# The shared expert moves beside the choice of experts, and each expert's tile is scaled and added to the result's rows by an indirect transfer

## Chip, cores and metric

The kernel runs on one core of one Trainium2 chip. The metric is the device time of one execution in microseconds.

## The reference

A block of a transformer on 4 x 512 tokens of 512 values, all in float32. With `x` the tokens after a gated attention, which this change does not touch, the second half is a mixture of experts:

```
xn = layernorm(x)                                  # 2048 tokens x 512
scores = softmax(xn @ Wg.T)                        # 16 experts
keep the 2 best of 4 groups of experts, then the 4 best experts of those (weights = their scores)
y = sum over the 4 chosen experts of weight * (silu(xn @ W1.T) * (xn @ W3.T)) @ W2.T   # inner width 352
z = (silu(xn @ Ws1.T) * (xn @ Ws3.T)) @ Ws2.T      # shared expert, every token, inner width 704
out = x + tanh(g_ffn) * (y + z)
```

## The kernel before, in words

The stages follow each other, each in a block of its own that all engines leave before the next begins: projections and attention (0 to 596 us of the profile), then four that matter here.

`stage_close` (to 739 us) works in four batches of 512 tokens. SyncE loads the attention's output and its denominators (`c_den`), VectorE normalises, TensorE projects (L689), VectorE makes `x1` (L658) and the layer norm's `x2` (L673), TensorE transposes `x2` (L697) and makes the 16 logits per token. GpSimd's queue stores `x1` (L603), `x2` (L606) and, once both have landed, the transposed tokens `xT` (L610) to DRAM.

`stage_route` (739 to 809) is one long chain on VectorE with a wait after each instruction: softmax, best groups, best experts (`MAX8` per 128 tokens), and a place for each chosen pair of token and expert. The pairs are sorted by expert, each expert is padded to tiles of 128 rows, 79 tiles in all. Two small matmuls count (L918, L919). 64 matmuls (L927) with 79 columns each write the table `token` (which token stands in which row of which tile), from masks that VectorE makes. `slot` and `weight` say for each token where its four results will stand, and their weights.

`stage_experts` (809 to 1415) loops over the 79 tiles of 128 rows. GpSimd gathers the rows of `x2` four tiles ahead by an indirect transfer (L1071, after a copy of the tile's indices, L1068). TensorE transposes them (L1172), ScalarE rounds them to float32r and copies them (L1108, L1109), GpSimd subtracts to get the low part (L1076). Every product is made in three passes, high x high, high x low and low x high: `gate` and `up` (L1181, twelve matmuls each), the transposition of `h` (L1188), `yps` (L1200, nine). GpSimd also multiplies silu(gate) by up (L1088) and makes the low part of `h` (L1080). ScalarE copies the tile (L1121) and stores it to DRAM as `dy` (L1125). The weights of an expert (1.97 MB) are loaded by SyncE into one of two buffers once the last tile of the expert before the last is done (L1015 to L1019), and VectorE splits them into a high and a low part in nine pieces (L1044 to L1052). In its last part the stage also loads and splits the shared expert's weights (L1058, L1060).

`stage_combine` (1415 to the end) computes the shared expert in four batches: twelve matmuls for `gate` and twelve for `up` for each of six chunks of the inner width (L1375), then for each of four tiles of 128 tokens eighteen matmuls into `yps` (L1384). ScalarE and VectorE make `h` (L1311, L1331 to L1335). GpSimd gathers the four expert results of each token by indirect transfers (L1294). VectorE sums them with their weights, scales by tanh(g_ffn), adds `x1` (L1346, L1349), and SyncE stores a batch.

## Time and profile before

| | |
|---|---|
| median of three runs | 1698.18 us (1687.57 to 1803.11) |
| the profiled execution | 1688.83 us, of which its span is 1686.8 us |
| mean granted clock of TensorE | 0.870 of full speed |
| TensorE busy | 1348.6 us (80%) |
| VectorE, ScalarE, GpSimd busy | 755.0, 533.9, 613.2 us |
| moved | 194.97 MB |

"Busy" is the time in which at least one instruction of the engine runs. A granted clock of 1.0 is 2.4 GHz and one of 0.5 is 1.2 GHz. A stretch's clock is a mean over time, so 0.76 is a mix of the two levels. All times of rows count from the span's start.

### The profile page before, as it was taken

The numbers are of one execution on the slowest core, as the hardware profiler recorded it, in microseconds if no ns is written. First come the engines' busy times: TensorE is split into PE (matmuls) and PEld (weight loads), VectorE is DVE, ScalarE is ACT, GpSimd is POOL, SyncE is SP. The second block draws the span as 40 slices with busy tenths as digits, with TensorE's granted clock in tenths as the row PEclk, the third lists the DMA queues.
The fourth block names the chain that finished last, engine by engine and source line by source line (L and its number), as shares of the span: only waits on it lengthen the run. The fifth ranks groups of instructions, "written<-read, shape, count | busy, mean of one in ns | idle before, by whom it ended". The sixth has DMA issues, their size and how long they took to land. (4 is left out here: it accounts for less than half of the span.)

```text
span 1686.8 us, 28607 instructions
## 1 busy us (share of the span) xinstructions
PE 1348.6 (80%) x8380; PEld 965.6 (57%) x8381; DVE 755.0 (45%) x1939; ACT 533.9 (32%) x951; POOL 613.2 (36%) x810
## 2 busy tenths in 40 slices
PE   6566089889989836735399999999989995999996
PEld 3233064333333313435399998988888884675673
DVE  2112047888787314458503533443353520344343
ACT  1101015555555500110155554544444442100100
POOL 4111002333332200000267776775666774042232
PEclk9877589999898767855699999998999997998897
DMA  5434222333232154620344444443533533052342
GB/s 184 129 118 137 86 72 68 91 97 98 71 99 77 42 171 153 221 102 0 133 128 126 132 132 159 137 126 109 175 113 113 194 103 137 13 175 66 109 148 75
DMA packets 100017, 194.97 MB, mean 116 GB/s; under 512 B 27044, under 2 KB 28580, under 8 KB 98952
## 3 DMA queue, kind: packets, MB, share of 16 engines
q1 hardware_dynamic: 71400, 118.35, 21.9%
q0 software_dynamic: 17200, 55.38, 11.2%
q10 hardware_dynamic: 11376, 20.71, 3.2%
q8 instruction: 23, 0.38, 0.1%
q14 instruction: 18, 0.15, 0.0%
HBM read 130.07 MB, written 64.03 MB: 115 GB/s over the span
## 5 line engine op out<-in xcount | busy, mean ns | idle before, releaser
L421 DVE CUSTOM_DVE_ANT_0 a_mb<-a_mb,late 128x384 f32<-128x384 f32 (+3 forms) x512 | 244.1, 513 | 109.6 <-PE a_mb L458 102.2
L1044 DVE CAST e_w<-e_w 128x480 fp32r<-128x480 f32 x144 | 99.2, 699 | 319.2 <-DMA e_w<-in_w2T 319.1
L400 ACT ACTIVATE a_at<-a_eb 128x1024 f32<-128x1024 f32 (+3 forms) x256 | 178.5, 705 | 179.1 <-PE a_eb L476 179.1
L344 POOL TENSOR_SCALAR_AFFINE_SELECT a_at<-a_at 128x256 f32<-128x256 f32 x256 | 104.5, 408 | 331.1 <-ACT a_at L400 331.1
L1181 PE MATMUL e_gate<-e_w,e_xT 128*128 x948 | 178.0, 339 | 39.0 <-DVE e_w L1052 34.6
L1181 PEld LDWEIGHTS e_gate<-e_w,e_xT 128*128 128x128 f32 x948 | 165.2, 200 | 50.6 <-issue 39.8
L1200 PE MATMUL e_yps<-e_w,e_hT 128*128 x711 | 185.5, 404 | 1.9 <-ACT e_hT L1113 1.4
L1181 PE MATMUL e_up<-e_w,e_xT 128*128 x948 | 174.7, 334 | 0.0
L1181 PEld LDWEIGHTS e_up<-e_w,e_xT 128*128 128x128 f32 x948 | 154.2, 193 | 0.0
L490 PE MATMUL a_pv<-a_at,a_v 128*32 128x256 f32 (+3 forms) x2048 | 133.1, 335 | 14.5 <-POOL a_at L344 8.6
L1200 PEld LDWEIGHTS e_yps<-e_w,e_hT 128*128 128x128 f32 x711 | 128.1, 189 | 27.3 <-issue 1.6
L458 PE MATMUL a_mb<-a_k,a_q 49*128 49x256 f32 (+2 forms) x512 | 114.0, 442 | 14.1 <-DVE a_mx L421 4.1
L1080 POOL TENSOR_TENSOR e_hT<-e_hc,e_hT 128x384 fp32r<-128x384 f32 x79 | 86.1, 1090 | 101.3 <-ACT e_hc L1114 101.0
L1071 POOL DMA_INDIRECT e_x<-dx,e_idx x79 | 94.6, 1197 | 62.5 <-POOL e_idx L1068 62.5
L1048 DVE TENSOR_TENSOR e_w<-e_w 128x480 fp32r<-128x480 f32 x128 | 116.7, 912 | 0.0
L1076 POOL TENSOR_TENSOR e_xT<-e_xc,e_xT 128x512 fp32r<-128x512 f32 x79 | 109.8, 1390 | 8.8 <-ACT e_xc L1109 2.4
L1384 PE MATMUL s_yps<-ws,s_h 128*128 128x512 f32 (+1 forms) x288 | 103.7, 497 | 10.9 <-DVE s_h L1335 8.3
L476 PE MATMUL a_eb<-a_q,a_k 50*128 50x512 f32 x512 | 112.1, 434 | 0.0
L458 PEld LDWEIGHTS a_mb<-a_k,a_q 49*128 49x128 f32 x512 | 49.6, 190 | 94.7 <-DVE a_mx L421 87.7
L689 PE MATMUL c_op<-c_wo,c_on 128*128 128x512 f32 x128 | 61.6, 643 | 50.6 <-DVE c_on L637 29.9
L490 PEld LDWEIGHTS a_pv<-a_at,a_v 128*32 128x32 f32 x2048 | 42.5, 112 | 100.7 <-POOL a_at L344 54.5
L1088 POOL TENSOR_TENSOR e_h<-e_act,e_upc 128x352 f32<-128x352 f32 x79 | 83.4, 1056 | 32.1 <-ACT e_upc L1138 29.8
(194 smaller groups left out, 1785.7 us busy)
## 6 DMA issues: line engine op xcount, KB each, us to landing
e_w<-in_w13T SPq DMA_DIRECT2D x16, 1408.0 KB
dy<-e_y ACTq DMA_DIRECT2D x79, 256.0 KB
dq<-p_parts SPq DMA_DIRECT2D x48, 256.0 KB
a_q<-dq SPq DMA_DIRECT2D x64, 192.0 KB
do<-a_o SPq DMA_DIRECT2D x32, 256.0 KB, 3.5
dx<-c_x POOLq DMA_DIRECT2D x8, 1024.0 KB, 8.2
e_w<-in_w2T SPq DMA_DIRECT2D x16, 512.0 KB
a_k<-dk SPq DMA_DIRECT2D x64, 98.0 KB
```

The source lines that it names most:

```text
L344: eng.affine_select(out=square, in_=square, compare_op=ALU.is_ge, fill=0.0, base=0, pattern=[[0, 2], [1, P]], channel_multiplier=-1).then_ ...
L400: eng.activation(at[r % 2][:, ch, 2 * hp:2 * hp + 2, ch * P:SEQ], eb[hp][:, :, ch * P:SEQ], ACT.Exp, scale=0.25).then_inc(s_exp, 1)
L421: eng.tensor_tensor_reduce(out=b[:, 0:w], in0=b[:, 0:w], in1=io["late"][:, SEQ - w:SEQ], scale=1.0, scalar=3 * NEG, op0=ALU.add, op1=ALU.m ...
L458: eng.matmul(bank(place(turn, j, t))[:, 0:w], q[r][rows, j, ch * P:(ch + 1) * P], k[r][rows, 0:w], start=True, stop=True).then_inc(s_smax, 1)
L476: mm = eng.matmul(eb[j][:, t], k[r][rows, ch * P:(ch + 1) * P], q[r][rows, j, :], start=True, stop=True)
L490: mm = eng.matmul(pv[32 * h:32 * h + 32, cols], v[r][:, ch, :], at[r % 2][:, ch, 2 * j + t, cols], start=ch == 0 and part == 0, stop=ch == ...
L1044: eng.tensor_copy(w[rows, r, 0, cols], w[rows, r, 1, cols].bitcast(F32)).then_inc(s_high, 1)
L1048: eng.tensor_tensor(w[rows, r, 1, cols], w[rows, r, 1, cols].bitcast(F32), w[rows, r, 0, cols].bitcast(F32), ALU.subtract).then_inc(s_low, 1)
L1076: eng.tensor_tensor(xT[r][:, 1], xc[:], xT[r][:, 0].bitcast(F32), ALU.subtract).then_inc(s_xlow, 1)
L1181: mm = eng.matmul(out[r][:], xT[r][:, mine, k, :], w[:, bass.ds(buf, 1), its, at:at + INTER].rearrange("p b n -> p (b n)"), start=not (min ...
L1200: mm = eng.matmul(yps[:], hT[r][0:size, mine, n, :], w[0:size, bass.ds(buf, 1), its, at:at + D].rearrange("p b n -> p (b n)"), start=not ( ...
L1384: mm = eng.matmul(yps[j % 2][:], h[0:size, mine, n, j * P:(j + 1) * P], w2[0:size, its, n, :], start=not (mine or its or n), stop=mine == ...
```

## The change

- In `stage_close` ScalarE's queue loads the shared expert's three weight matrices, one after each of the first batches; ScalarE rounds each (`high_weights`), and GpSimd subtracts to get the low part (`low_weights`), behind the batch's stores.
- `stage_route` and `stage_combine` become one, `stage_shared`. VectorE runs the routing chain. TensorE computes the shared expert, with the two counting matmuls after the sixth chunk and the matmuls of the table two groups at a time after chunks 7 to 14. These now carry 158 columns, since the table holds the token and the scaled weight. In the down product the first five chunks of two result tiles come before the sixth. What VectorE did for the shared expert is done by ScalarE (`upc`, `h` high) and GpSimd (product, low parts, sum with `x1`). `x1 + tanh(g) * z` is stored to `out` in tiles of 256 KB. SyncE loads the first expert's weights at the stage's start, and the second's after all of these stores have landed. VectorE splits the first expert's weights at its chain's end.
- In `stage_experts` ScalarE scales each tile by its rows' weights as it copies it (`io["scale"]`), and GpSimd adds it to the rows of `out` with an indirect transfer that adds at its destination (`scatter`). That of tile g waits until that of g-1 has landed. Rows of padding go to 128 rows behind the result. GpSimd's loop is written out for all 79 tiles, without the copies of indices. The store of `dy`, the four gathers per token and the sums over four experts are gone. `y` has four buffers instead of two.

The core of the diff:

```diff
+def load_expert(eng, io, e, buf):
+
+    raw = io["w"][:, buf, SIDE:].bitcast(F32)
+    eng.dma_start(raw[:, 0:W13].rearrange("p (c n) -> p c n", c=KD),
+                  io["w13T"][bass.ds(e, 1)].rearrange("e (c p) n -> p (e c) n", p=P)).then_inc(io["s_w"], 16)
+    eng.dma_start(raw[:, W13:FULL].rearrange("p (c n) -> p c n", c=NI - 1),
+                  io["w2T"][bass.ds(e, 1), 0:(NI - 1) * P].rearrange("e (c p) n -> p (e c) n", p=P)).then_inc(io["s_w"], 16)
+    eng.dma_start(raw[0:REST, FULL:], io["w2T"][bass.ds(e, 1), (NI - 1) * P:INTER].rearrange("e p n -> (e p) n")).then_inc(io["s_w"], 16)
+
...
+            def high_weights(n):
+                high, _, raw = weights[n]
+                eng.wait_ge(s_ws, 16 * WS[n])
+                if n < 2:
+                    eng.activation(high, raw.bitcast(F32), ACT.Copy).then_inc(s_whigh, 1)
+                else:
...
+            eng.wait_ge(s_eps, 2)
+            for b in range(BATCH):
+                eng.wait_ge(s_mv, (b + 1) * CH + 1)
+                eng.activation(root[:], mv[:, :, 1], ACT.Sqrt, bias=eps[:]).then_inc(s_root, 1)
+                eng.wait_ge(s_keptT, b + 1)
+                for j in range(CH):
+                    eng.wait_ge(s_tr, b * CH + j + 2)
+                    eng.activation(x2T[:, :, j * P:(j + 1) * P], tp[j % 2][:], ACT.Copy).then_inc(s_xT, 1)
+                eng.wait_ge(s_lg, b + 2)
+                eng.activation(io["logits"][:, bass.ts(b, CH), :], lp[:], ACT.Copy).then_inc(s_lc, 1)
+                if b < 3:
+                    high_weights(b)
+                if b < 2:
+                    load_weights(b + 1)
...
+            def low_weights(n):
+                eng.wait_ge(s_whigh, n + 2)
+                high, low, raw = weights[n]
+                for rows, cols in ([(slice(0, P), slice(k * SHARED, (k + 1) * SHARED)) for k in range(KD)] if n < 2 else
+                                   [(slice(0, P), slice(k * D, (k + 1) * D)) for k in range(NS - 1)]):
+                    eng.tensor_tensor(low[rows, cols], raw[rows, cols].bitcast(F32), high[rows, cols].bitcast(F32), ALU.subtract).then_inc(s_wlow, 1)
...
+            for b in range(BATCH):
                 eng.wait_ge(s_x1, (b + 1) * CH + 1)
...
+                if b < 3:
+                    low_weights(b)
...
+            eng.tensor_scalar(indexf[:], tokps[:, 0:TILES], pad[:, 0:1], None, ALU.add).then_inc(s_v, 1)
...
+            eng.tensor_copy(io["scale"], tokps[:, TILES:]).then_inc(s_v, 1)
...
+            eng.wait_ge(io["s_w"], LOAD)
+            w = io["w"]
+            for n in range(CUTS + 1):
+                p, cols = cut(n)
+                eng.tensor_copy(w[p, 0, cols], w[p, 0, SIDE + cols.start:SIDE + cols.stop].bitcast(F32)).then_inc(s_high, 1)
+                eng.wait_ge(s_high, n + 2)
+                eng.tensor_tensor(w[p, 0, SIDE + cols.start:SIDE + cols.stop], w[p, 0, SIDE + cols.start:SIDE + cols.stop].bitcast(F32),
+                                  w[p, 0, cols].bitcast(F32), ALU.subtract).then_inc(s_low, 1)
 
...
+            def result(b, j):
+                i = b * CH + j
+                eng.wait_ge(s_down, i + 2)
+                if i >= 2:
+                    eng.wait_ge(s_sum, i)
+                eng.activation(part[i % 2][:], yps[i % 2][:], ACT.Copy, scale=tg[:, 0:1]).then_inc(s_part, 1)
...
+            for i, (b, n) in enumerate(units):
+                size = SCH[n][1]
+                eng.wait_ge(s_gate, i + 2)
+                eng.activation(act[i % 2][0:size], gate[i % 2][0:size], ACT.Silu).then_inc(s_act, 1)
+                eng.wait_ge(s_up, i + 2)
+                eng.activation(upc[i % 2][0:size], up[i % 2][0:size], ACT.Copy).then_inc(s_upc, 1)
+                eng.wait_ge(s_raw, i + 2)
+                if n == 0 and b:
+                    eng.wait_ge(s_down, b * CH + 1)
+                eng.activation(h[0:size, 0, n, :], raw[i % 2][0:size], ACT.Copy).then_inc(s_hhigh, 1)
+                if n == NS - 1:
+                    for j in range(CH):
+                        result(b, j)
+                        if j == 0 and b + 1 < BATCH:
+                            high_x(b + 1)
 
...
+            def add(b, j):
+                i = b * CH + j
+                eng.wait_ge(s_part, i + 2)
+                if j == 0:
+                    eng.wait_ge(s_x1, 16 * (b + 1))
+                eng.tensor_tensor(x1[:, j, :], part[i % 2][:], x1[:, j, :], ALU.add).then_inc(s_sum, 1)
+
+            low_x(0)
+            for i, (b, n) in enumerate(units):
+                size = SCH[n][1]
+                eng.wait_ge(s_act, i + 2)
+                eng.wait_ge(s_upc, i + 2)
+                eng.tensor_tensor(raw[i % 2][0:size], act[i % 2][0:size], upc[i % 2][0:size], ALU.mult).then_inc(s_raw, 1)
+                eng.wait_ge(s_hhigh, i + 2)
+                eng.tensor_tensor(h[0:size, 1, n, :], raw[i % 2][0:size], h[0:size, 0, n, :].bitcast(F32), ALU.subtract).then_inc(s_hlow, 1)
+                if n == NS - 1:
+                    for j in range(CH):
+                        add(b, j)
+                        if j == 0 and b + 1 < BATCH:
...
+            def multiply(i, n, m, out, done):
+                at, size = SCH[n]
+                for mine, its in PASSES:
+                    if mine and n == 0 and m == 0:
+                        eng.wait_ge(s_xlow, i // NS + 2)
+                    for k in range(KD):
+                        mm = eng.matmul(out[i % 2][0:size], weights[m][its][:, k * SHARED + at:k * SHARED + at + size],
+                                        xT[:, bass.ds(side[mine], 1), k, :].rearrange("p b n -> p (b n)"),
+                                        start=not (mine or its or k), stop=mine == 1 and k == KD - 1)
+                mm.then_inc(done, 1)
+
+            def down(b, j, chunks):
+                i = b * CH + j
+                for mine, its in PASSES:
+                    for n in chunks:
+                        size = SCH[n][1]
+                        first = its * DOWN + n * D
+                        mm = eng.matmul(yps[i % 2][:], h[0:size, mine, n, j * P:(j + 1) * P],
+                                        io["w"][0:size, bass.ds(side[1], 1), first:first + D].rearrange("p b n -> p (b n)"),
+                                        start=not (mine or its or n), stop=mine == 1 and n == NS - 1, skip_group_check=True)
...
+            def table(t):
+                r = t % 2
+                eng.wait_ge(s_row, 3 * t + 4)
+                for k in range(NK):
+                    mm = eng.matmul(tokps[:], at_row[r][:, k, :], at_col[r][:, k].rearrange("p n g -> p (n g)"), start=t == 0 and k == 0,
+                                    stop=t == NT - 1 and k == NK - 1, skip_group_check=True)
+                mm.then_inc(s_tok, 1)
+
+            for i, (b, n) in enumerate(units):
+                if n == 0:
+                    eng.wait_ge(s_xhigh, b + 2)
+                if i >= 2:
+                    eng.wait_ge(s_act, i)
+                multiply(i, n, 0, gate, s_gate)
+                if i >= 2:
+                    eng.wait_ge(s_upc, i)
+                multiply(i, n, 1, up, s_up)
+                if i == NS - 1:
+                    eng.wait_ge(s_ch, 2)
+                    eng.matmul(flat(within), io["before"], flat(chosen[:]), start=True, stop=True).then_inc(s_mm, 1)
+                    eng.matmul(flat(totals), io["onesb"], flat(chosen[:]), start=True, stop=True).then_inc(s_mm, 1)
+                if NS <= i < NS + NT // 2:
+                    for t in range(2 * (i - NS), 2 * (i - NS) + 2):
+                        table(t)
+                if n == NS - 1:
+                    early, late = tuple(range(NS - 1)), (NS - 1,)
+                    eng.wait_ge(s_hlow, i + 1)
+                    for j in range(2):
+                        if b or j >= 2:
+                            eng.wait_ge(s_part, b * CH + j)
+                        down(b, j, early)
+                    eng.wait_ge(s_hlow, i + 2)
+                    for j in range(2):
+                        down(b, j, late)
+                    for j in range(2, CH):
+                        eng.wait_ge(s_part, b * CH + j)
+                        down(b, j, early + late)
+
+        @block.sync
+        def _(eng):
+            def load_xT(b):
...
+            load_xT(0)
+            eng.dma_start(gf[:], io["gf"].broadcast_to([P, 1])).then_inc(s_g, 16)
+            load_expert(eng, io, 0, 0)
+            for b in range(BATCH):
+                if b:
+                    eng.wait_ge(io["s_base"], 16 * CH * b)
+                eng.dma_start(x1, dram["x1"][bass.ts(b, SEQ), :].rearrange("(j p) d -> p j d", p=P)).then_inc(s_x1, 16)
+                eng.wait_ge(s_up, (b + 1) * NS + 1)
+                if b + 1 < BATCH:
+                    load_xT(b + 1)
+                for j in range(CH):
+                    eng.wait_ge(s_sum, b * CH + j + 2)
+                    eng.dma_start(out[bass.ts(b * CH + j, P), :], x1[:, j, :]).then_inc(io["s_base"], 16)
+            eng.wait_ge(s_down, NT + 1)
+            eng.wait_ge(io["s_base"], 16 * NT)
+            load_expert(eng, io, 1, 1)
...
+            def gather(g):
+                n = g % XB
+                eng.indirect_dma_start(out=x[n][:], out_offset=None, in_=dram["x2"],
+                                       in_offset=bass.IndirectOffsetOnAxis(ap=io["gather"][:, g:g + 1], axis=0)).then_inc(s_x[n], 16)
+
+            def scatter(g):
+                n, last = g % XB, (g - 1) % XB
+                eng.wait_ge(s_y, g + 2)
+                if g:
+                    eng.wait_ge(s_out[last], 16 * ((g - 1) // XB + 1))
+                else:
+                    eng.wait_ge(io["s_base"], 16 * NT)
+                eng.indirect_dma_start(out=out, out_offset=bass.IndirectOffsetOnAxis(ap=io["scatter"][:, g:g + 1], axis=0),
+                                       in_=y[n][:], in_offset=None, compute_op=ALU.add).then_inc(s_out[n], 16)
 
...
+            for g in range(TILES):
+                r = g % 2
+                if g:
                     low_h(g - 1, 1 - r)
                 eng.wait_ge(s_upc, g + 2)
                 eng.wait_ge(s_act, g + 2)
                 eng.tensor_tensor(h[r][:, 0:INTER], act[r][:], upc[:], ALU.mult).then_inc(s_h, 1)
-                if exists(g + 1):
+                if g < LAST:
                     low_x(g + 1, 1 - r)
-                if exists(g + XB):
+                if g >= 2:
+                    scatter(g - 2)
+                if g + XB < TILES:
                     eng.wait_ge(s_xt, g + 2)
-                    gather(g + XB, n)
-
-            for g in range(XB):
-                gather(g, g)
-            for r in range(2):
-                eng.memset(h[r][:, INTER:], 0.0).then_inc(s_pad, 1)
...
+                eng.activation(y[n][:], yps[:], ACT.Copy, scale=io["scale"][:, bass.ds(g, 1)]).then_inc(s_y, 1)
```

## Rows read from the trace of the kernel before

The times in a timeline are start and duration in us; in brackets stands how long the engine sat idle before, and what ended it. In the table by stage the columns are the window, its length, each engine's busy us (instructions), the granted clock, the DMA engines' share and GB/s.

**Rows 1.** Table by stage: close, route, experts, combine.

```profile
607.00:739.00 132.00, 90.20 (x320) 53.05 (x320) 52.37 (x116) 16.33 (x29) 8.31 (x12) 0.77 0.51 185
739.00:809.00 70.00, 28.55 (x132) 28.06 (x132) 56.71 (x224) 1.70 (x2) 0.67 (x5) 0.50 0.00 0
829.00:1415.00 586.00, 550.02 (x3156) 509.58 (x3156) 216.94 (x279) 272.06 (x551) 388.43 (x386) 0.97 0.39 128
1427.00:1687.00 260.00, 237.20 (x864) 163.62 (x864) 112.65 (x156) 19.83 (x28) 64.72 (x73) 0.89 0.32 105
```

**Rows 2.** Timeline, end of the routing stage.

```profile
807.81 0.24 DVE L906 CAST token<-r_tokps 128x79 int32<-128x79 f32 x1
```

**Rows 3.** Timeline, start of the experts' stage.

```profile
811.67 1.06 POOL L1071 DMA_INDIRECT e_x<-dx,e_idx  x1 [0.94 <-POOL e_idx L1068]
...
818.91 1.11 PE L1172 MATMUL e_xps<-ident,e_x 128*128 128x128 f32 x4 [13.84 <-DMA e_x<-dx,e_idx]
...
829.50 0.95 PE L1181 MATMUL e_gate<-e_w,e_xT 128*128 x2 [9.47 <-DVE e_w L1052]
```

**Rows 4.** Table of waits, closing stage: total us, times, longest.

```profile
DVE c_on L637 <- DMA c_den<-dinv: 54.9, 3, 19.1
```

**Rows 5.** Timeline of GpSimd around one tile of the experts.

```profile
1007.79 1.01 POOL L1071 DMA_INDIRECT e_x<-dx,e_idx  x1 [0.79 <-POOL e_idx L1068]
1009.93 1.01 POOL L1080 TENSOR_TENSOR e_hT<-e_hc,e_hT 128x384 fp32r<-128x384 f32 x1 [1.12 <-ACT e_hc L1114]
...
1012.30 1.29 POOL L1076 TENSOR_TENSOR e_xT<-e_xc,e_xT 128x512 fp32r<-128x512 f32 x1
...
1014.51 1.01 POOL L1071 DMA_INDIRECT e_x<-dx,e_idx  x1 [0.79 <-POOL e_idx L1068]
```

**Rows 6.** Timeline, one load and split of an expert's weights.

```profile
1013.43 0.38 SPq L1015 DMA_DIRECT2D e_w<-in_w13T  x1
...
1023.82 1.14 DVE L1044 CAST e_w<-e_w 128x480 fp32r<-128x480 f32 x2 [20.14 <-DMA e_w<-in_w2T]
...
1026.20 1.50 DVE L1044 CAST e_w<-e_w 128x480 fp32r<-128x480 f32 x1
...
1028.19 0.40 DVE L1044 CAST e_w<-e_w 128x480 fp32r<-128x480 f32 x1
...
1037.21 1.08 PE L1181 MATMUL e_gate<-e_w,e_xT 128*128 x5 [3.88 <-DVE e_w L1052]
```

**Rows 7.** Table of waits, experts' stage.

```profile
PE e_gate L1181 <- DVE e_w L1052: 34.6, 8, 9.5
```

**Rows 8.** Timeline of GpSimd, end of the closing stage.

```profile
724.70 0.75 POOL L603 DMA_DIRECT2D dx<-c_x  x1 [4.66 <-issue]
...
735.20 0.55 POOL L610 DMA_DIRECT2D dxT<-c_x2T  x1 [4.65 <-DMA dx<-c_x]
```

**Rows 9.** Chain that ended last, order of time, last stage: start, us, what.

```profile
1418.73 6.35 DMA s_gf<-in_gf
...
1427.15 4.67 PE s_gate L1375 x12
...
1434.54 2.72 PE s_gate L1375 x12
...
1523.34 27.29 PE s_yps L1384 x72
...
1674.46 3.68 DMA s_got<-dy,s_idx
```

**Rows 10.** Table by windows, one down phase of the shared expert.

```profile
1523.00:1551.00 28.00, 27.66 (x74) 16.07 (x75) 13.65 (x17) 0.01 (x1) 8.74 (x10) 0.76 0.24 65
```

**Rows 11.** Groups of instructions, last stage, TensorE.

```profile
L1384 PE MATMUL s_yps<-ws,s_h 128*128 128x512 f32 (+1 forms) x288 | 103.7, 497 | 10.9 <-DVE s_h L1335 8.3 <-DVE s_h L1333 2.6
```

**Rows 12.** DMA issues: median us to landing last.

```profile
do<-a_o SPq DMA_DIRECT2D x32, 256.0 KB, 3.5
```

**Rows 13.** Timeline of ScalarE, end of the experts' stage.

```profile
1411.02 0.60 ACT L1121 ACTIVATE e_y<-e_yps 128x512 f32<-128x512 f32 x1 [2.15 <-PE e_yps L1200]
```

500 lines of the change are left out of this document (189 added, 311 removed).

## The prediction

> **What bounds the kernel now.** I read the stretches by stage first, then the waits inside each, then a few timelines. In the table by stage [rows 1] the reader is to see that TensorE is nearly always busy in the experts' stage (550 of 586 us) and in the last stage, which holds the shared expert and the combination (237 of 260 us), and nearly idle in the routing stage (28.6 of 70 us, at half the clock). So the time of the two big stages is the time of their matmuls, and the 70 us of routing are a chain of small VectorE instructions that hides nothing. Its last instruction, the copy of the table of tokens, comes at 807.81, 69 us into the stage [rows 2]. Behind it the first gather needs from 811.67 to 818.91 to land, and the first expert's gate waits until 829.50 for split weights [rows 3]. The stage before routing waits for transfers [rows 4].
>
> In the experts' stage the rhythm is that of one tile: two gathers start 6.72 us apart [rows 5]. Seven times, besides the start, an expert's weights come late: loading starts at 1013.43, has landed at 1023.82, and the gate that uses it starts at 1037.21 after 3.88 us of idleness [rows 6]; with the start it is 34.6 us in 8 waits [rows 7].
>
> **The change, part by part.** The sum is made against the profiled span, 1686.8 us.
>
> *Closing stage: +14.* The shared weights are now loaded (4.1 MB), rounded by ScalarE and split by GpSimd in this stage. The loads compete with the reads for which VectorE already waits 54.9 us in three batches [rows 4]. At the 185 GB/s of this stretch [rows 1] 4.1 MB are 22 us if all of it lay on the path; nothing if it fits between. I take 4. The third split stands on GpSimd ahead of the last batch's two stores. It is five pieces of 128x512 and one smaller, at 1.29 us each [rows 5] 7.7 us, behind ScalarE's rounding, some 2 us more. The store that went out at 724.70 [rows 8] goes out at about 734.5, and the last one of the stage, at 735.20, depends on it. That is +10; zero would need another cover, and I see none, since GpSimd was already the last to issue. Bounds for the part: 0 to +25.
>
> *Routing and start of the experts: −90.5.* From 739 to 829.5 nothing of the old order is left on TensorE's path. VectorE's chain runs beside the shared expert. It needs its 70 us, some 15 us more for the waits for TensorE (the counting matmul now stands behind the sixth chunk), and a split of 9 us, and has 250. The longest cover in this change is that one; if it failed, the tables would come late and TensorE would stand.
>
> *The shared expert in its new place: +250.6.* Stage start 3 us, then 10 us until transposed tokens are loaded and rounded: in the old stage the first loads were under way at 1418.73 and the gate starts at 1427.15 [rows 9]. 48 groups of twelve matmuls at 2.72 us [rows 9] are 130.6, plus 2 for the first at the low clock (4.67 instead of 2.72). The down phase took 27.3 us for 72 matmuls [rows 9], at a mean granted clock of 0.76 [rows 10]: half of it at 1.2 GHz, and each of the four begins after 2.7 us of idleness, 10.9 in all [rows 11]. The new order puts the first five chunks of two result tiles in front, so that this idleness goes; at the full clock the phase is 27.3 x 0.76 = 20.7 us, four are 83. If the clock stays as it was, they are 109. The table matmuls move in here: 128 instructions took about 28 us at half the clock [rows 1]. They now carry 158 columns instead of 79. Between 14 (twice the clock) and 28 I take 20, with 2 for small waits. Sum: 13 + 130.6 + 2 + 83 + 20 + 2.
>
> GpSimd now does the shared expert's product and its low part, 2 x 1.29 us in each 5.44 us of a chunk, and ScalarE three passes; both are hidden. Rows show that VectorE and GpSimd slow each other: the same cast takes 1.50 us at 1026.20 and 0.40 at 1028.19 [rows 6]. The Trainium skill, "SBUF — State Buffer", section "Who interferes with whom", says that a VectorE instruction with two SBUF inputs contends with GpSimd's reads, and this change puts routing beside GpSimd's work on purpose. By that rule doubled GpSimd times would be 5.2 of 5.44 us in a chunk, still covered, and the first split of the tokens would come about 5 us later: the sum would be 5 us higher. I leave it out, since the row behind it is of another mix.
>
> *Handing over to the experts: +18.7.* After TensorE's last matmul come scaling (0.6, as the copy in [rows 13]), the addition (1.3 [rows 5]), a store of 256 KB, which in this profile lands after 3.5 us [rows 12], its issue and those of the second expert's load (1.7), because SyncE waits for all stores before it issues that, and the next stage's start (2.6). Then the gather's 7.2 us [rows 3] and 1.8 to a rounded tile. The first expert's weights are split by then, which is why the 10 us between 818.91 and 829.50 go.
>
> *The experts' loop: 581.5 becomes 606.5.* On ScalarE the issue of the store disappears. On GpSimd the copy of an index and the 0.79 us for which the gather waits for it [rows 5] disappear, and one indirect transfer of 1.01 us comes. Issue alone is about even. New is the wait in front of it: the scatter of tile g−2 waits until that of g−3 has landed. Behind it on GpSimd stand the gather four tiles ahead and the low part of h, for which TensorE's down product waits. GpSimd waits 1.12 us for ScalarE there today [rows 5], so with the slack behind it a scatter may take some 8 us from its issue once, but in the long run no more than the 6.72 of a tile. No row shows an adding transfer. The nearest are an indirect read of the same size, landed 3.68 us after its issue at the end [rows 9], and 7.2 us beside a weight load [rows 3]. With reading and writing of its destination I put it at 5 to 5.5 alone and 9 to 10 beside a load. Alone it is hidden; beside each of 14 loads one or two lie over the limit, about 1 us each time after the slack: 15. The destination is read too, so the load itself lasts longer, about 1.4 us, and seven experts already wait for theirs: 10. Bounds: 0 (both hidden) to several hundred (the rival below).
>
> The Trainium skill, "DMA: Bandwidth & Descriptors", section "Anatomy of one DMA", fits a GpSimd transfer as 2.0 us plus bytes over 436e3, which is 2.6 us for 256 KB; it has no figure for an adding one. With that the 15 us would vanish and the sum be 15 lower; the trace's 3.68 is already longer.
>
> *The end: 275.8 removed, 9 added.* From TensorE's last expert matmul, for which ScalarE waits until 1411.02 [rows 13], to the end stood the whole last stage. Now: the last tile is scaled (0.6), the scatter before it must have landed, then its own issue and landing, 1 + 5.5, and the stage's close.
>
> Sum: 739 + 14 + 250.6 + 18.7 + 606.5 + 9 = 1637.8. Outside the span the profiled run had 2.0 us, so 1640. The profiled run (1688.8) is near the lowest of the three shown and 0.6% below their median, 1698.2; a median of the new kernel may lie as much above its own profile. Halfway between, I say 1645. A measurement of this kernel can tell about 2% from no change.
>
> **The rivals.**
> *The chain of scatters sets the pace (slower).* Each scatter waits for the one before, so if one takes L us from issue to landing and L is over 6.72, the tile takes L. At 8.7 us, 79 tiles cost 158 us, of which 25 are counted: 1640 + 133 = 1773. For it: the transfers must read, add and write 2 KB rows, and beside loads even a plain gather took 7.2. Against it: 3.68 us alone, and a plain 256 KB store 3.5. It decides exactly at 6.72 us. 0.16.
>
> *The weights come too late everywhere (no change).* If the adding transfers lengthen every load by 5 us, seven short experts wait 5 more, and the seven of five tiles or more, which have about 3.5 us to spare (four tiles at 6.72, less 10.4 of loading and 13 of splitting), wait 1.5 and run 1.6 at the low clock: some 57, of which 10 are counted: 1687. For it: 10.4 of the about 27 us between loading and use go to the load already. 0.15.
>
> *The overlap is worse than it looks (no change).* The down phase stays at 0.76 (+26) and the tables at 28 (+8): 1674. Against it: the idleness in front of the phase, after which the clock was low, is filled. 0.04.
>
> *Everything hidden (faster still).* No cost in the closing stage and none in the loop: 1640 − 14 − 25 = 1601. 0.20.
>
> **How the numbers follow.** The forecast, 1625 to 1665, gets 0.45. A tenth of it lies within 2%. Faster by over 2%: 0.40 + 0.20 = 0.60. Within 2%: 0.05 + 0.15 + 0.04, about 0.23. Slower: 0.17, the chain. The range is 1595 to 1720; it leaves out the chain and a little of the edges.
>
> **What would show it.** Right: TensorE busy from about 765 to 1005 with the clock near full in the down phases, VectorE's tables done before 920, experts' gates from about 1025, GpSimd's waits for a scatter only beside loads. Wrong: a tile's rhythm above 6.8 us with GpSimd's scatter waiting for the transfer each time; more than 4 us of waiting at each new expert; a closing stage that ends after 765; waits of TensorE for the tables.

## The result, and the profile after

The new kernel took **1645.14 us** (median of 4, 1636.26 to 1649.12), the kernel before 1694.57 (median of 4) on the same chip: ratio **0.9714**, 95% interval 0.965 to 0.9779. The ratio is of the fast executions alone; one of the kernel before, 1803.11 us, was slow. The profiled execution took 1647.19 us with a span of 1645.3. A second series on another chip gave 1649.14, ratio 0.9796 (0.9725 to 0.9867): faster too, but by an amount that its interval puts between 1.3 and 2.8%.

The profile was read like that of before: stages, then what ends the waits in each. Table by stage, new kernel: close, shared expert beside the choice, experts (columns as in [rows 1]).

```profile
600.00:753.00 153.00, 92.13 (x320) 53.84 (x320) 62.61 (x116) 19.98 (x30) 30.80 (x26) 0.72 0.53 187
763.00:1004.00 241.00, 233.42 (x994) 174.01 (x994) 104.53 (x224) 63.37 (x95) 102.13 (x68) 0.97 0.16 56
1017.00:1632.00 615.00, 564.41 (x3156) 513.49 (x3156) 210.49 (x265) 272.79 (x553) 476.19 (x390) 0.95 0.50 115
```

The two stretches that [rows 1] shows as routing (70 us, TensorE 28.6 busy) and last stage (260) are one of 241 us in which TensorE is busy for 233. In the experts' stage, against [rows 1], GpSimd's busy time has gone from 388 to 476 us of some 600 and TensorE's clock from 0.97 to 0.95, and the stage has grown by 30 us: that is the row to explain.

GpSimd at the end of the closing stage, timeline; it answers to [rows 8].

```profile
734.94 6.14 POOL L677 TENSOR_TENSOR e_w<-e_w 128x512 fp32r<-128x512 f32 x5 [6.20 <-ACT e_w L649]
741.05 1.44 POOL L681 TENSOR_TENSOR e_w<-e_w 64x512 fp32r<-64x512 f32 x1
742.44 0.79 POOL L686 DMA_DIRECT2D dx<-c_x  x1
...
750.11 0.55 POOL L692 DMA_DIRECT2D dxT<-c_x2T  x1 [5.15 <-DMA dx<-c_x]
```

The third split stands for 7.6 us ahead of the store, which is issued 17.7 us later than in [rows 8], the last one 14.9 later. But the two profiles don't start the stage at the same time. Its first load, kernel before and new kernel, timeline:

```profile
593.76 0.34 SPq L579 DMA_DIRECT2D c_sums<-do  x1
587.10 0.34 SPq L613 DMA_DIRECT2D c_sums<-do  x1
```

The work ahead of the stage, which the change does not touch, was 6.7 us shorter in the new kernel's profile. From this load to the last store it is 141.4 us before and 163.0 after: the closing stage has grown by 21.6 us, and 14.9 is what is left of it on the clock of the span. The wait of [rows 4], new kernel:

```profile
DVE c_on L706 <- DMA c_den<-dinv: 78.7, 4, 22.3
```

A down phase of the shared expert, new kernel, table by windows: clock 1.00, where [rows 10] had 0.76. TensorE's 72 matmuls take 19.5 us instead of 27.3.

```profile
929.00:949.50 20.50, 20.41 (x78) 13.55 (x77) 0.00 (x0) 5.54 (x7) 10.94 (x6) 1.00 0.25 90
```

From the shared expert to the first expert, timeline, new kernel; it answers to [rows 3].

```profile
1002.07 0.69 ACT L1035 ACTIVATE s_part<-s_yps,s_tg 128x512 f32<-128x512 f32 x1 [4.67 <-PE s_yps L1118]
...
1010.67 1.06 POOL L1270 DMA_INDIRECT e_x<-dx,gather  x1 [6.58 <-POOLq L75]
...
1015.78 1.12 PE L1375 MATMUL e_xps<-ident,e_x 128*128 128x128 f32 x4 [13.75 <-DMA e_x<-dx,gather]
...
1017.78 2.71 PE L1384 MATMUL e_gate<-e_w,e_xT 128*128 x8 [0.88 <-DVE e_w L1259]
...
1018.16 5.71 POOL L1285 TENSOR_TENSOR e_xT<-e_xc,e_xT 128x512 fp32r<-128x512 f32 x1 [2.44 <-ACT e_xc L1322]
...
1023.93 1.54 PE L1384 MATMUL e_gate<-e_w,e_xT 128*128 x4 [3.44 <-POOL e_xT L1285]
```

The gather ends a wait of 13.75 us, and then GpSimd's low part, 5.71 us instead of 1.3 while VectorE splits weights, holds the gate's last matmuls up for 3.44 us.

GpSimd around one tile of the experts, timeline, new kernel; it answers to [rows 5].

```profile
1206.62 1.02 POOL L1289 TENSOR_TENSOR e_hT<-e_hc,e_hT 128x384 fp32r<-128x384 f32 x1
1207.59 0.94 POOL L1303 TENSOR_TENSOR e_h<-e_act,e_upc 128x352 f32<-128x352 f32 x1
1208.49 1.27 POOL L1285 TENSOR_TENSOR e_xT<-e_xc,e_xT 128x512 fp32r<-128x512 f32 x1
1209.93 1.59 POOL L1280 DMA_INDIRECT out<-e_y,scatter  x1 [0.17 <-issue]
1211.83 1.00 POOL L1270 DMA_INDIRECT e_x<-dx,gather  x1 [0.30 <-issue]
...
1225.36 1.72 POOL L1280 DMA_INDIRECT out<-e_y,scatter  x1 [2.48 <-DMA out<-e_y,scatter]
```

In [rows 5] GpSimd waited 1.12 us for ScalarE and 0.79 for an index; over the stage it was 101.0 us in 69 tiles and 59.2 in 75. Here the five instructions follow each other with at most 0.3 us between them: this tile of 6.7 us is full. Over the whole loop GpSimd is busy for 78%, and it still waits 33.0 us for ScalarE ahead of the low part of h, in 17 tiles. The scatter's issue takes 1.59 us, and beside a load it waited 2.48 for the one before it.

The table of waits in the experts' stage (against [rows 7]):

```profile
POOL out L1280 <- DMA out<-e_y,scatter: 38.3, 14, 3.0
PE e_gate L1384 <- DVE e_w L1259: 19.9, 8, 4.5
PE e_yps L1403 <- POOL e_hT L1289: 17.3, 14, 1.4
```

TensorE waits less for weights (19.9 us; 34.6 before) and in exchange for the low part of h, which stands behind the scatter. The tiles that this touches are those beside a load. Taken between starts of GpSimd's product, half of all tiles are no longer than 6.72 us, in the kernel before (6.71) as in the new one; but 30 are over 7.2 us, where it was 10. A late split, timeline (against [rows 6]):

```profile
1228.11 4.29 DVE L1259 TENSOR_TENSOR e_w<-e_w 128x480 fp32r<-128x480 f32 x1
...
1234.99 3.81 DVE L1250 CAST e_w<-e_w 128x480 fp32r<-128x480 f32 x1
...
1242.41 3.88 PE L1384 MATMUL e_gate<-e_w,e_xT 128*128 x12 [4.49 <-DVE e_w L1259]
```

Two of VectorE's instructions take some 4 us instead of 0.40 and 0.65. Each covers one unbroken run of GpSimd's three arithmetic instructions (from 1228.77 to 1231.88, and from 1235.40 to 1238.52; such a run fills 1206.62 to 1209.76 above). The 14 whole splits of the loop take 14.6 us in the mean, where they took 13.5. The end, timeline, and the summary of all scatters:

```profile
1629.84 0.69 ACT L1334 ACTIVATE e_y<-e_yps,scale 128x512 f32<-128x512 f32 x1 [2.17 <-PE e_yps L1403]
1631.60 1.57 POOL L1280 DMA_INDIRECT out<-e_y,scatter  x1 [2.84 <-DMA out<-e_y,scatter]
1637.15 1.57 POOL L1280 DMA_INDIRECT out<-e_y,scatter  x1 [3.98 <-DMA out<-e_y,scatter]
```

```profile
L1280 POOL DMA_INDIRECT out<-e_y,scatter x79: 1568/1595/1861, 1044.9 to 1637.1; - x79
...
DMA to landing us min/median/max: 4.6/4.9/8.8
```

### The profile page after: what moved, and what is told of

It is laid out like the page before. It is cut to its first block and busy times, and to the rows that moved or that the text cites. A ratio compares the mean times of both kernels' runs of the same rounds, so it can differ in the third digit from the quotient of the medians.

```text
span 1645.3 us, 27429 instructions
## 1 busy us (share of the span) xinstructions
PE 1324.6 (81%) x8378; PEld 949.2 (58%) x8379; DVE 689.4 (42%) x1765; ACT 577.0 (35%) x1016; POOL 755.5 (46%) x812
## 5 line engine op out<-in xcount | busy, mean ns | idle before, releaser
L1250 DVE CAST e_w<-e_w 128x480 fp32r<-128x480 f32 x135 | 93.7, 703 | 421.4 <-DMA e_w<-in_w2T 421.4
L1384 PE MATMUL e_gate<-e_w,e_xT 128*128 x948 | 184.1, 346 | 30.2 <-DVE e_w L1259 19.9
L1403 PE MATMUL e_yps<-e_w,e_hT 128*128 x711 | 189.1, 407 | 18.3 <-POOL e_hT L1289 17.3
L1384 PEld LDWEIGHTS e_gate<-e_w,e_xT 128*128 128x128 f32 x948 | 167.5, 203 | 46.9 <-issue 37.4
L1280 POOL DMA_INDIRECT out<-e_y,scatter x79 | 130.7, 1654 | 56.1 <-DMA out<-e_y,scatter 42.3
L521 PE MATMUL a_pv<-a_at,a_v 128*32 128x256 f32 (+3 forms) x2048 | 129.6, 327 | 15.1 <-POOL a_at L375 8.6
L1259 DVE TENSOR_TENSOR e_w<-e_w 128x480 fp32r<-128x480 f32 x135 | 136.6, 1020 | 0.0
L1270 POOL DMA_INDIRECT e_x<-dx,gather x79 | 85.1, 1077 | 30.0 <-issue 22.1
L1289 POOL TENSOR_TENSOR e_hT<-e_hc,e_hT 128x384 fp32r<-128x384 f32 x79 | 81.5, 1031 | 34.3 <-ACT e_hc L1327 33.0
L1334 ACT ACTIVATE e_y<-e_yps,scale 128x512 f32<-128x512 f32 x79 | 54.4, 689 | 112.9 <-PE e_yps L1403 112.9
```

The lines of the kernel that those rows point to most:

```text
L521: mm = eng.matmul(pv[32 * h:32 * h + 32, cols], v[r][:, ch, :], at[r % 2][:, ch, 2 * j + t, cols], start=ch == 0 and part == 0, stop=ch == ...
L1250: eng.tensor_copy(w[rows, r, cols], w[rows, r, SIDE + cols.start:SIDE + cols.stop].bitcast(F32)).then_inc(s_high, 1)
L1259: eng.tensor_tensor(w[rows, r, rest], w[rows, r, rest].bitcast(F32), w[rows, r, cols].bitcast(F32), ALU.subtract).then_inc(s_low, 1)
L1280: eng.indirect_dma_start(out=out, out_offset=bass.IndirectOffsetOnAxis(ap=io["scatter"][:, g:g + 1], axis=0), in_=y[n][:], in_offset=None, ...
L1384: mm = eng.matmul(out[r][:], xT[r][:, mine, k, :], w[:, bass.ds(buf, 1), its * SIDE + at:its * SIDE + at + INTER].rearrange("p b n -> p (b ...
L1403: mm = eng.matmul(yps[:], hT[r][0:size, mine, n, :], w[0:size, bass.ds(buf, 1), its * SIDE + at:its * SIDE + at + D].rearrange("p b n -> p ...
```

## The experiments

Profiled executions differ by up to 28 us in when the closing stage starts, in work that no experiment touches. So stretches are compared: *shared* is from TensorE's first gate of the shared expert to its last down matmul, *loop* from the first expert's first gate to the last down matmul, *handover* between these, *tail* from the loop's end to the span's. Each is taken between starts of matmuls. Loops of kernels with the same loop came out between 604 and 614 us; less than 10 us there is no verdict. Most experiments ran once. Four of them (e2, e3, e4, e7) leave out, or do twice, a part of the result's sum, and e10 works with stale low parts: they measure and are no kernels to keep.

| run | shared | handover | loop | tail | time (runs) |
|---|---|---|---|---|---|
| the changed kernel | 234.1 | 16.3 | 611.6 | 15.9 | 1645.14 (4) |
| a0_new | 233.9 | 16.3 | 611.0 | 14.8 | 1649.14 (4) |
| e1_tables_first | 212.1 | 16.4 | 608.1 | 14.6 | 1690.23 (1) |
| e5_down_in_order | 271.3 | 16.4 | 604.1 | 14.5 | 1673.90 (1) |
| e6_split_last | 234.5 | 16.3 | 604.3 | 14.6 | 1643.51 (5) |
| e8_gather_early | 232.3 | 10.6 | 610.9 | 14.4 | 1655.07 (1) |
| e2_two_results | 234.5 | 17.0 | 594.1 | 9.4 | 1623.46 (1) |
| e3_plain_store | 234.0 | 16.4 | 588.4 | 6.1 | 1624.74 (1) |
| e4_twice | 232.2 | 16.4 | 894.5 | 30.5 | 1953.97 (1) |
| e7_no_add | 232.2 | 16.4 | 590.5 | 11.0 | 1638.97 (1) |
| e10_less_low | 232.3 | 16.3 | 580.4 | 14.8 | 1616.80 (1) |
| e11_scatter_earlier | 232.2 | 16.4 | 647.1 | 13.4 | 1692.64 (10) |
| e9_both | 232.3 | 10.6 | 614.3 | 14.6 | 1640.74 (6) |

The kernel before had a loop of 581.1.

**The changed kernel again** (a0_new), beside the first experiments.

> The new kernel again, on the chip of the next three. Both theories: within 0.5% of its first profile, a span of 1637 to 1653 us. The stretches to compare with: closing stage until its last store is issued at 750, shared expert's matmuls from 767 to 1002, the experts' from 1018 to 1630.

It agreed in every stretch, to 1.1 us.

**Is hiding the route the gain?** (e1_tables_first)

```
     for i in range(NS + NT // 2 ...):      # TensorE's units of the shared expert
-        if i == NS - 1: wait s_ch; matmul within, totals
-        if NS <= i ...: table(t)
+    # all of it ahead of the loop: wait s_ch; matmul within, totals; table(t) for t in range(NT)
```

> TensorE makes the counts and the whole table before the first chunk of the shared expert, so that the routing chain again stands in front of everything. Theory (the gain is mainly the chain of small VectorE instructions, now hidden): TensorE starts the shared expert 75 to 85 us later, saves the 19 us of table matmuls among the chunks, and the time rises by 55 to 65 us, to about 1705, nearly all of the way back to the kernel before. Rival (the gain comes from the gathers, sums and idle gaps of the old last stage, and the chain would cost little): under 20 us.

TensorE started the shared expert 66.5 us later than in a0_new (837.1 against 770.6), the shared stretch shrank by 21.8, and the first expert's gate came 44.8 us later. The rival, under 20, fell; the theory was some 10 too high. The overlap is worth about 45 us, as much as the whole gain of the change. Of the 21.8 us only some 17 are the tables' matmuls. The rest is the start of the shared expert: its first two groups of twelve take 6.69 and 3.95 us behind idleness in the changed kernel, and 3.06 and 2.96 here, behind the tables.

**Does the order of the down phase keep the clock?** (e5_down_in_order)

```
-  early, late = tuple(range(NS - 1)), (NS - 1,)
-  wait s_hlow i+1;  down(b, 0, early), down(b, 1, early);  wait s_hlow i+2;  late of 0, 1;  then 2, 3
+  wait s_hlow i+2;  down(b, j, tuple(range(NS))) for j in 0..3
```

> The down product of the shared expert takes its six chunks in order for each tile, with no early part in front of the wait for the last chunk. Theory: TensorE idles some 4 us before each of the four down phases (two passes on ScalarE and two on GpSimd), the granted clock of the phase falls to about 0.76 as in the kernel before, and each batch costs 4 + 6 us: +35 to +42 in all. Rival (the clock is not lost through that gap, the old phases were slow for another reason, as the sums on VectorE): only the gaps, +14 to +18, and a clock above 0.9 in the phases.

The shared stretch grew by 37.4 us, as the theory had it. Table by windows, the third down phase of this run with the wait ahead of it:

```profile
941.00:970.00 29.00, 24.93 (x75) 14.55 (x75) 0.00 (x0) 5.39 (x7) 10.89 (x6) 0.88 0.17 63
```

The third phase itself and the last one, timeline of this run:

```profile
945.17 24.48 PE L1118 MATMUL s_yps<-e_w,s_h 128*128 x72 [4.07 <-POOL s_h L1084]
1007.50 30.04 PE L1118 MATMUL s_yps<-e_w,s_h 128*128 x72 [4.07 <-POOL s_h L1084]
```

TensorE waited 14.1 us for the last chunk's h in four waits, and was busy 23 us longer over the whole stage (256.4 against 233.4) for the same matmuls at a lower clock. The four waits were 3.9, 2.0, 4.07 and 4.07 us, and the phases behind them took 23.0, 23.0, 24.5 and 30.0 us, at a mean granted clock of 0.93, 0.93, 0.86 and 0.67; in the changed kernel each takes 19.5 or 19.6. So a wait and its phase together cost 9 us in the mean, but from 5 to 15, and the 0.76 of the theory is not one value that every phase has.

**The split ahead of the stores** (e6_split_last)

```
     after batch b's stores of dx and dxT:
-    if b < 3: low_weights(b)
+    if b < 2: low_weights(b)
+    if b == 3: low_weights(2)       # behind the last store of dxT
```

> The split of the third shared matrix on GpSimd stands behind the last batch's stores in the closing stage, not in front of them. Theory (it is that split that makes the stage end some 9 us later): the last store of the stage goes out 8 us earlier and the whole gains 6 to 9 us, about 0.5%. Rival (the added weight loads and the slowed VectorE set the end of the stage): 0 to 2 us.

From the stage's first matmul to the last store of dxT it is 129.0 us instead of 133.8 in the changed kernel (127.9 in e9_both), but from there to the shared expert's gate 21.3 instead of 17.3 (20.7 in e9_both). Together it is 150.3 us, and 148.6 in e9_both, where the kernels whose closing stage is as in the changed one lie between 150.2 and 154.1: a gain of 3 us at most, and in e6 none that can be told. Timeline of this run, what stands there now:

```profile
768.02 0.55 POOL L692 DMA_DIRECT2D dxT<-c_x2T  x1 [4.38 <-DMA dx<-c_x]
768.59 6.14 POOL L677 TENSOR_TENSOR e_w<-e_w 128x512 fp32r<-128x512 f32 x5
774.69 1.25 POOL L681 TENSOR_TENSOR e_w<-e_w 64x512 fp32r<-64x512 f32 x1
779.81 0.34 SPq L1167 DMA_DIRECT2D s_xT<-dxT  x1
```

The next stage's first load goes out at 779.81, 11.8 us behind the last store instead of 8.1 in the changed kernel: the split is now the last work that the block of the closing stage has to wait for. In total 1643.51, ratio 0.9732 (0.9664 to 0.9799), not to be told from the changed kernel. The expected 6 to 9 was a miss.

**The gather in the handover** (e8_gather_early)

```
+  # stage_shared, GpSimd, behind the addition of the last batch's second tile:
+  wait s_low 2;  four gathers into io["ex"] (x laid over shared weights no longer used)
+  # VectorE: wait s_xlow 2 ahead of the second expert's split;  gathers leave the experts' stage
```

> The first four gathers are issued by GpSimd in the shared stage, behind its second last additions, into a part of the shared weights that is dead by then, and VectorE's split of the second expert waits until the first tile's low part is made. Theory (the handover of 16 us between the last down product and the first gate holds 5 us of gather latency and its queueing, and the first low part takes 5.7 instead of 1.3 us beside the split): the first gate starts 4 to 6 us earlier and the second pass does not wait 3.4 us, -7 to -10 us. Rival (the store and the load in front of the stage's end are the handover, the gather hides behind them): 0 to 3 us.

The handover is 5.7 us shorter, the 4 to 6 of the theory's first half; the wait on VectorE gave nothing more, since another of the first tiles' low parts came late instead (TensorE waited 4.2 us in all). The single time of 1655.07 says nothing of this: its closing stage started 16 us later than in the changed kernel.

**Who pays in the experts' loop: two destinations** (e2_two_results)

```
-  wait scatter(g - 1) landed;  out=out
+  wait scatter(g - 2) landed;  out=dram["out2"] if g % 2 else out     # base stored to both
```

> Scatters of odd tiles go to a second array of the result's shape, which is not added to the result; each scatter waits for the last but one and not for the one before. The base is stored to both. Theory (beside a weight load a scatter lands after 8.8 us, over the 6.7 of a tile, and GpSimd's wait for it delays the low part of h): the 17 us that TensorE waits for that low part vanish, and the loop shortens by 14 to 22 us, with the splits of weights unchanged. Rival (GpSimd is late by its work, 1.6 us for each scatter, and the wait only fills the gap): under 5 us.

Waits of TensorE, this kernel, loop:

```profile
PE e_gate L1386 <- DVE e_w L1260: 37.3, 10, 5.5
...
PE e_yps L1405 <- POOL e_hT L1291: 0.4, 1, 0.4
```

GpSimd's wait for a landing is gone and so is TensorE's for the low part of h (17.3 to 0.4); the loop is 17 us shorter, as the theory had it, and the rival fell. The scatter still takes 1.59 us to issue, and the splits are as long as before or longer (14.8 us). The tiles over 7.2 us go from 30 to 13. Weights come late more often (37.3 us against 19.9): part of what TensorE waits for the low part of h in the changed kernel comes back here as waiting for weights.

**No scatters** (e3_plain_store)

```
-  GpSimd: scatter(g - 2)
+  ScalarE: dma_start(dram["y"][tile g], y[n])          # as before
```

> No scatter: each scaled tile is stored in order to an array of its own from ScalarE's queue, as in the kernel before, and not added to the result. This measures all that the scatters cost in the loop. Theory (32 us longer than before, through waits of GpSimd and through VectorE's splits, which last 14.9 instead of 13.6 us beside a busier GpSimd): the experts' loop takes 580 to 585 us as before, splits 13.6, and 8 us more are saved at the end, -35 to -42 in all. Rival (the loop is longer for another reason, such as instructions written out 79 times or the first tiles): the loop stays above 600.

Loop −23 and tail −10, so −33 where −35 to −42 was expected; splits take 12.6 us. The other 7 us of the loop against the kernel before are not the scatter, and too few to be told from nothing. Beside e2 this says one thing more: without the wait for landings the loop is 594.1 us, and without the scatter altogether 588.4. The issue of 79 scatters, 1.60 us each, is worth 6 us of the loop at most, less than the 10 that can be told.

**Two scatters per tile** (e4_twice)

```
+  again(g - 3) behind low_h:  wait s_out 32*(..)+16;  the same adding transfer a second time
```

> Each tile is added twice, the second time by a scatter that waits for the first and for which the next tile's first one waits. It stands between the two products of GpSimd. Theory (the chain of scatters is hidden as long as it is shorter than a tile and sets the pace above that): a tile takes twice 4.9 us and a little, 9.8 to 10.5, the loop 775 to 830 us, +160 to +220. Rival (scatters overlap in part or only their issue counts): 1.6 us more a tile at most, +130 or less.

GpSimd in two tiles of this kernel, timeline:

```profile
1300.82 1.59 POOL L1280 DMA_INDIRECT out<-e_y,scatter  x1 [1.85 <-DMA out<-e_y,scatter]
...
1305.97 1.58 POOL L1286 DMA_INDIRECT out<-e_y,scatter  x1 [1.21 <-DMA out<-e_y,scatter]
...
1311.50 1.59 POOL L1280 DMA_INDIRECT out<-e_y,scatter  x1 [1.78 <-DMA out<-e_y,scatter]
```

These start 5.2 and 5.5 us behind the one before. In the loop all but one of the scatters waited for the landing of the one before; from start to start it is 5.4 us in the middle and 5.7 in the mean, and up to 11 beside loads. The tile takes 11.3 us in the mean, and the kernel 1954. Both theories were below that (the loop 283 us longer instead of 160 to 220). So a chain of scatters does set the pace once it is longer than a tile. With one scatter per tile of 6.7 us and a link of 5.4 to 5.7 the prediction's rival is about 1 us away. The second scatter also stands in the place that e11 below shows to be a bad one, so not all of the 283 us need be the chain's.

**What adding costs** (e7_no_add)

```
-  in_=y[n][:], in_offset=None, compute_op=ALU.add)
+  in_=y[n][:], in_offset=None)
```

> The same scatters in the same chain, which overwrite the rows and do not add. Theory (reading the destination is a small part of the 4.9 us, issue and landing the rest): landing 3.7 to 4.4 us alone and 7 to 8 beside a load, issue still 1.6; the loop 3 to 12 us shorter. Rival (the adding form is what makes both issue and landing slow): issue falls to the gather's 1.0 us, landing to 3.7, the loop gains 20 us or more.

Summary of this kernel's scatters:

```profile
L1280 POOL DMA_INDIRECT out<-e_y,scatter x79: 968/1029/1284, 1062.9 to 1629.4; - x79
...
DMA to landing us min/median/max: 2.7/2.8/7.2
```

The adding form costs 0.57 us more to issue and 2.1 more to land. The loop falls by 20.5 us, the rival's size; my theory that this part is small fell. It is no more than 4 us beyond e2, which kept the slow issue.

**Is it the landing, or is GpSimd full?** e3 and e7 shorten both the issue and the landing; e2 took away the wait alone. This one gives GpSimd time and leaves the scatters alone (e10_less_low).

```
   # low_x, from the third tile on
-  tensor_tensor(xT[r][:, 1], xc, xT[r][:, 0], subtract)
+  some = slice(0, 1);  tensor_tensor(xT[r][:, 1, some], xc[:, some], xT[r][:, 0, some], subtract)
```

> From the third tile on, GpSimd makes only a quarter of the tokens' low part (128x128 instead of 128x512; the rest stays what it was two tiles earlier); scatters, their waits and everything on the other engines stay. GpSimd gets back some 1.0 us of each 6.7 us tile. Theory (GpSimd has no slack: between 1199.2 and 1221.6 of the changed kernel its five instructions follow each other with waits of 0.3 us at most, so that the 1.60 us issue of a scatter, not only its landing, is what fills the engine, and what a landing takes is not won back): the loop falls from 611 to 592 to 600 us, TensorE's waits for the low part of h from 19 to under 8. Rival (only the landing beside a load counts, and VectorE's splits): the loop stays within 5 us of 611, with the same waits of GpSimd for the landing and TensorE's waits for the low part of h as before, 15 to 20.

Table of waits, this kernel, loop:

```profile
POOL e_hT L1290 <- ACT e_hc L1328: 54.3, 50, 4.5
POOL out L1280 <- DMA out<-e_y,scatter: 35.7, 13, 3.1
PE e_gate L1385 <- DVE e_w L1259: 24.1, 13, 3.0
...
PE e_yps L1404 <- POOL e_hT L1290: 4.3, 13, 0.6
```

The loop takes **580.4 us, that of the kernel before**, while GpSimd waits for landings as long as it did (35.7 us in 13 waits; 35.5 in 13 in the changed kernel's loop). What changed is that GpSimd waits for ScalarE again (54.3 us; 33.0 in the changed kernel, 101.0 before), so a late landing is won back before TensorE needs the low part of h. So a late landing alone costs nothing; it costs where GpSimd has no time to win it back. The theory had this, but not the size: the loop fell by 31 us and not by 11 to 19. The splits also went from 14.6 to 13.2 us, and the clock from 0.95 to 0.98. Half of the 31 us is TensorE's idleness (47.6 to 32.2 us), half its busy time (564.4 to 548.5): the granted clock is at its low level for 17 us of this loop, for 38 in the kernel before, and for 51 to 56 in the changed kernel, in e2, in e7 and in e3, which has no scatter at all. The run takes off arithmetic that the kernel before had too (0.8 us of GpSimd per tile, measured, not the 1.0 expected), so its 31 us are not the price of the scatter. How much of them is time won back and how much VectorE's shorter splits it doesn't separate.

**Where the scatter stands** (e11_scatter_earlier)

```
   for g: low_h(g - 1)
+         scatter(g - 2)
          product(g);  low_x(g + 1)
-         scatter(g - 2)
          gather(g + 4)
```

> Only the order on GpSimd changes: the scatter of tile g-2 stands behind the low part of h of tile g-1 and ahead of the product of tile g, instead of behind the low part of the next tokens. What then stands behind a late landing is the product, for which a transposition waits, and no longer the low part of h. Theory (the in-line position decides whom a late landing holds up): TensorE's waits for the low part of h fall from 19 to under 8, those for the product rise by less than that, and the loop is 3 to 10 us shorter than 611. Rival (GpSimd has no slack wherever the scatter stands, so that a wait of 2 to 3 us arrives at TensorE in any order): the waits only change their name, and the loop stays at 605 to 615, the time within 0.5% of the changed kernel's.

Both theories fell, though TensorE's waits for the low part of h are gone as the first had it: the loop is 36 us longer, and the kernel is back at the time of before (ratio 0.9985, 0.9944 to 1.0026). Its waits, and GpSimd in one tile:

```profile
POOL e_hT L1289 <- ACT e_hc L1327: 131.9, 79, 7.4
PE e_gate L1384 <- POOL e_xT L1285: 42.6, 63, 2.5
```

```profile
1215.21 1.48 POOL L1289 TENSOR_TENSOR e_hT<-e_hc,e_hT 128x384 fp32r<-128x384 f32 x1 [0.91 <-ACT e_hc L1327]
1216.85 1.59 POOL L1280 DMA_INDIRECT out<-e_y,scatter  x1 [0.16 <-issue]
1217.92 1.50 POOL L1305 TENSOR_TENSOR e_h<-e_act,e_upc 128x352 f32<-128x352 f32 x1
1218.83 1.82 POOL L1285 TENSOR_TENSOR e_xT<-e_xc,e_xT 128x512 fp32r<-128x512 f32 x1
```

GpSimd isn't even full here, it waits 0.9 us or more for ScalarE in every tile. By its waits, the scatter now stands inside a ring: low part of h, product, low part of the next tokens, then TensorE's gate, which waits for it in 63 of 79 tiles. In the changed kernel the scatter stands behind the low part of the tokens, where only the gather follows, which is four tiles early. The same instructions in another order on one engine cost 36 us of loop.

**The two mends together** (e9_both: e6 and e8)

> The late split in the closing stage and the early gathers together. Theory: the gains add up, -13 to -18 us, 0.8 to 1.1% faster than the new kernel. Rival: one of them hides the other or comes to nothing, under 0.5%.

1640.74 us, ratio 0.9745 (0.97 to 0.9791). The handover kept its 5.7 us and the closing stretch its 3, but the total can't be told from the changed kernel's, and the 13 to 18 us did not come.

## Why the prediction came out as it did

By its own terms, ends measured against the predicted ones (stage ends taken as the prediction took them, the closing stage 3.8 us behind its last store):

| term | predicted | measured |
|---|---|---|
| closing stage | +14 | +14.9 |
| shared expert in its new place | 250.6 | 248.2 |
| handover | 18.7 | 15.7 |
| experts' loop | 606.5 | 612.1 |
| end | 9 | 15.5 |
| span | 1637.8 | 1645.3 |

*Closing stage: right on the span's clock by luck.* Against its own start the stage has grown by 21.6 us, not 14.9, since the work ahead of it was 6.7 us shorter in this profile. The split ahead of the stores is 7.6 us, as worked out, but taking it away shortens the stretch up to the last store by only 5 to 6 us, and the next stage starts at most 3 us earlier (e6, e9). So most of the 21.6 is not the split: from the first matmul to the last store it was 116.6 us before, 133.8 in the changed kernel, and still 129.0 in e6. For the competition of the weight loads I took 4 us (of 0 to 22), and this is the term with the largest miss of this part. That it is the loads is read from VectorE's wait for `c_den`, 78.7 us for 54.9, since the weight loads are what is new on the queues beside it; no run took them away.

*Shared expert: right in sum and in mechanism, its parts less so.* Tables cost 18.5 us for 20. Down phases took 77.9 us for 83, at a clock of 1.00. The 48 groups of gate and up took 139 us for 132.6, because the first two ran at the low clock (6.69 and 3.95 us; 4.67 and 2.88 before). The 109 us for down phases that keep the old clock went by one phase; the four of the kernel before took 23.0, 27.3, 27.4 and 25.9 us, the 103.7 of [rows 11]. The mechanism, that the idleness ahead of the phase sets its clock, is shown by e5; that the route is hidden, by e1. The Trainium skill's rule on VectorE and GpSimd ("SBUF — State Buffer", section "Who interferes with whom"), which the prediction weighed and left out here, cost TensorE next to nothing in this stage: the gate waited 0.8 us for GpSimd's low part. The trace agrees with the rule itself, with VectorE as the one that waits. While GpSimd makes that low part (from 767.37, for 4.54 us), a small instruction of the routing chain takes 4.42 us, where one of the same form takes 0.21 at 774.3, and the chain has time for it. Timeline, new kernel:

```profile
767.56 4.42 DVE L883 TENSOR_TENSOR r_gtmp<-r_gm 128x48 f32<-128x48 f32 x1
```

*Handover: 3 us less.* From the gather's issue to the transposition it was 5.1 us, not the 7.2 of [rows 3]. That same rule does show right behind it, 5.71 us instead of 1.3 for the first low part, which my sum had nowhere; it lies in the loop, 3.4 us.

*The loop: the landings right, the loads wrong.* The sum had 25 us, 15 for landings and 10 for slower loads; the loop grew by 30.6. Landings of 4.9 us alone and 8.8 at most beside a load were as predicted (5 to 5.5, 9 to 10), and so was their path: TensorE's waits for the low part of h are 17.3 us for the 15 said, and e2, which takes the wait for landings away, shortens the loop by 17. The term that is wrong is the 10 for slower loads: loads are 0.6 us longer instead of 1.4, and TensorE waits 15 us less for weights, not 10 more. e2 shows why: once TensorE is not held up by the low part of h, its waits for weights rise from 19.9 to 37.3 us. In place of the 10 stand 7 to 13 us that are left without a wait (e2: 594.1, e3: 588.4, before: 581.1), of which the record doesn't show the cause.

"Issue alone is about even" was put too simply, though it is not what cost the time. An adding scatter takes 1.60 us to issue, not the 1.01 of a gather, and what it replaced was mostly idleness (59.2 us for indices; and the waits for ScalarE fell from 101.0 to 33.0). In tiles away from a load it is even: the middle tile is 6.72 us long, as before. But the idleness was the reserve that a late landing is won back from, and the "slack behind it" of the prediction was mostly gone. e10 gives some of it back, and the landings, as late as ever, cost TensorE 4.3 us instead of 17.3. So it takes both, a late landing and an engine without reserve. VectorE's splits, held by GpSimd's unbroken runs, take 14.6 us instead of 13.5; e2 is 17 us shorter with splits as long, so they are not the larger part. In all TensorE is 14 us longer busy (564 against 550, clock 0.95 for 0.97) and 16 longer idle.

*The end: 6.5 us more.* The prediction let the scatter before the last have landed for nothing. Two stand back to back, 5.55 us apart; from the last one's issue to the end it is 8.2.

*The number.* That 1645 was said and 1645.14 measured is luck to this precision. The forecast put 5 us for the median on top of its sum, where the measured median lies 2 us below its own profile; the shorter work ahead of the closing stage gave 6.7 us; and the parts above err in both directions. The parts from the closing stage on are 14 us over their sum.

*The rivals.* The chain did not decide, with 6.72 us against 5.4 to 5.7 for a link; e4 shows that it would have, and e11 that a place in the wrong ring costs 36 us without any longer transfer. "Weights too late everywhere" is excluded by the row of 19.9 us, "the overlap is worse than it looks" by the clock of 1.00 in the down phases, and "everything hidden" by the 21.6 us of the closing stage and the 30.6 of the loop.

What stays open: the 7 to 13 us by which the loops of e3 and e2 are longer than that of before, which is near what can be told; what the weight loads alone cost the closing stage; and whether a low part of x made elsewhere, all of it, would keep e10's gain, which wasn't tried.

## What to carry to other kernels

When an instruction is added to an engine that serves others, count its idleness per tile before and after and not only its busy share: what it waited for was the reserve that swallowed late transfers (e10). When two profiles are compared stage by stage, take each stage from its own start: here the work ahead of it differed by 6.7 us. Put an instruction that may wait behind the last one on its engine that anybody needs in this tile, and ahead of one that is early anyway. Idle stretches of a few microseconds ahead of a block of matmuls can cost more than their length, because the clock falls behind them: here waits of 2 to 4 us were followed by blocks that took 3.4 to 10.5 us longer (e5).

## What the runs showed of the hardware

- An indirect scatter of 128 rows of 2 KB that adds at its destination takes 1.60 us of GpSimd to issue and lands after 4.9 us (8.8 at most, beside a weight load); the same without adding takes 1.03 and 2.8 (7.2). Back to back, each waiting for the last, the adding ones start 5.4 us apart in the middle, 5.7 in the mean.
- A VectorE instruction can be held for the whole of an unbroken run of GpSimd's arithmetic: 4.29 and 3.81 us instead of 0.65 and 0.40. The other way round a 128x512 subtraction on GpSimd took 5.71 us instead of 1.3 while VectorE split weights.
- 72 matmuls of a down phase took 19.5 us at a clock of 1.00 without a wait ahead of them, 23.0 us (0.93) behind waits of 3.9 and of 2.0 us, and 24.5 (0.86) and 30.0 us (0.67) behind waits of 4.07.
